# Mamba stage: GpSimd multiplies its tile of u times B by a per-partition scalar, and takes that tile in states 7, 8 and 15 too

## What is computed

```python
dt = softplus(log_dt @ W_dt.T + b_dt)                 # per position and inner channel (512)
A_bar = exp(dt[..., None] * A)                        # 16 states per inner channel
Bu = dt[..., None] * B_coef[:, :, None, :] * xc[..., None]
def step(h, inp):
    Ab, bu, c = inp
    h = Ab * h + bu
    y = einsum('bds,bs->bd', h, c)
    return (h, y)
```

## Time and profile before

| | us |
|---|---|
| median of 3 runs | 3870.74 |
| lowest and highest | 3869.91, 3874.35 |
| span of the profiled execution | 3867.2 |
| stretch of the Mamba stage in it, by first and last instructions | about 1275 to 3085 |

### The profile page before, as it was taken

One profiled execution on the slowest core, in us unless ns is written; L12 is line 12 of the kernel. 1 busy time (PEld: TensorE's weight loads), 2 busy tenths in 40 slices (PEclk: granted clock), 3 DMA queues, 4 the chain that ended last, 5 costly groups with the idle time before them and its releaser, 6 DMA issues. The chain is left out here.

```text
span 3867.2 us, 75281 instructions
## 1 busy us (share of the span) xinstructions
PE 3312.9 (86%) x23360; PEld 2499.0 (65%) x23360; DVE 3139.9 (81%) x5227; ACT 2800.4 (72%) x5125; POOL 2652.0 (69%) x2858
## 2 busy tenths in 40 slices
PE   8996989889954789898898889888888879997887
PEld 5664666667532567776776767676766757775554
DVE  5665899945395899899899989989999859998886
ACT  2223787844475888888888888888888647776997
POOL 1222677720094799999898999989999836664666
PEclk9998999979976899999999999999999989998999
DMA  2111122251113111111111111111111112221111
GB/s 65 54 55 52 45 52 50 50 116 38 41 44 84 34 51 53 57 50 52 49 56 51 56 54 48 54 51 51 56 51 48 44 48 74 73 53 56 59 56 39
DMA packets 285550, 209.64 MB, mean 54 GB/s; under 512 B 131416, under 2 KB 249752, under 8 KB 285224
## 3 DMA queue, kind: packets, MB, share of 16 engines
q1 hardware_dynamic: 285224, 205.72, 19.0%
HBM read 149.18 MB, written 51.41 MB: 52 GB/s over the span
## 5 line engine op out<-in xcount | busy, mean ns | idle before, releaser
L2896 POOL TENSOR_TENSOR ma_ch<-ma_h,ma_crep 128x512 f32<-128x512 f32 x1024 | 1368.8, 1358 | 160.0 <-DVE ma_h L2998 147.5
L2998 DVE TENSOR_TENSOR_SCAN ma_h<-ma_a,ma_pbu 128x512 f32<-128x512 f32 x1024 | 1212.7, 1206 | 172.6 <-PE ma_pbu L2576 113.0
L2576 PE MATMUL ma_pbu<-ma_ident,ma_bu 128*128 128x128 f32 x4096 | 657.7, 285 | 203.1 <-DVE ma_h L2998 161.7
L2576 PEld LDWEIGHTS ma_pbu<-ma_ident,ma_bu 128*128 128x128 f32 x4096 | 478.9, 144 | 446.1 <-DVE ma_h L2998 317.5
L2783 ACT ACTIVATE ma_a<-ma_dt,ma_A 128x510 f32<-128x510 f32 x1024 | 653.5, 718 | 1.4 <-issue 1.4
L2585 PE MATMUL ma_py<-ma_ident,ma_ch 128*128 128x128 f32 x4096 | 625.0, 279 | 0.6 <-POOL ma_ch L2896 0.6
L2774 ACT ACTIVATE ma_bu<-ma_uT,ma_b_t 128x512 f32<-128x512 f32 x784 | 508.2, 719 | 14.4 <-PE ma_pbu L2576 12.2
L2585 PEld LDWEIGHTS ma_py<-ma_ident,ma_ch 128*128 128x128 f32 x4096 | 495.8, 145 | 0.9 <-POOL ma_ch L2896 0.8
L1576 POOL TENSOR_TENSOR xa_prob<-xa_e,xa_rec_head 128x616 f32<-128x616 f32 x128 | 155.5, 1216 | 126.7 <-DVE xa_rec_head L1668 114.7
L924 POOL TENSOR_TENSOR xa_prob<-xa_e,xa_rec_head 128x616 f32<-128x616 f32 x128 | 155.5, 1216 | 108.2 <-DVE xa_rec_head L1016 90.6
L362 POOL TENSOR_TENSOR la_veps<-la_mv,la_eps 128x2 f32<-128x2 f32 x32 | 6.2, 195 | 248.2 <-DVE la_mv L395 248.2
(11 more groups left out here) (373 smaller groups left out, 8041.2 us busy)
## 6 DMA issues: line engine op xcount, KB each, us to landing
ma_crep<-ma_ct_dram SPq DMA_DIRECT2D x256, 256.0 KB
xa_x<-act SPq DMA_DIRECT2D x64, 256.0 KB, 2.6
act<-xa_y SPq DMA_DIRECT2D x64, 256.0 KB, 2.2
la_x<-in_x SPq DMA_DIRECT2D x32, 256.0 KB, 2.7
act<-la_y SPq DMA_DIRECT2D x32, 256.0 KB
act<-ea_x SPq DMA_DIRECT2D x32, 256.0 KB, 4.0
ma_x<-act SPq DMA_DIRECT2D x16, 512.0 KB, 4.5
ma_xr<-act SPq DMA_DIRECT2D x16, 512.0 KB
```

The source lines that it names most:

```text
L2576: last = pe.transpose(pbu[c % 2][:, t * P:(t + 1) * P], bu[:, s % 2, t, c * P:(c + 1) * P], ident[:, :])
L2896: pool.tensor_tensor(ch[:, s % 2, c], h[:, s % 2, c], crep[:, s % 4, :], ALU.mult).then_inc(multiplied, 1)
L2998: dve.tensor_tensor_scan(out=h[:, s % 2, c, :], data0=a[:, s % 2, c, :], data1=pbu[c % 2][:, :], initial=0.0, op0=ALU.mult, op1=ALU.add).t ...
```

## The change

Three things are changed. GpSimd's tile is made by `tensor_scalar` with a scalar from memory (times a constant 1.0) and no longer by `tensor_tensor` with a broadcast operand. The three waits ahead of the tile now stand ahead of `times_c` (s, 0) and not between it and the tile. And the tables give tile work of states 7, 8 and 15 from DVE to GpSimd: DVE has four tiles a group where it had seven, GpSimd eleven where it had eight. ACT's tiles stay as they were, two or three or four a state.

```diff
-        DVE_TILES = {1: 1, 7: 2, 8: 1, 9: 1, 10: 1, 15: 1}
-        POOL_TILES = {2: 1, 3: 1, 4: 1, 5: 1, 6: 1, 9: 1, 10: 1, 11: 1}
+        DVE_TILES = {1: 1, 7: 1, 9: 1, 10: 1}
+        POOL_TILES = {2: 1, 3: 1, 4: 1, 5: 1, 6: 1, 7: 1, 8: 1, 9: 1, 10: 1, 11: 1, 15: 1}
...
-            def scale_tile(g, par, s):
+            def tile_may_be_scaled(g, s):
                 pool.wait_ge(uT_copied, IC * g + IC)
                 pool.wait_ge(b_copied, g + 1)
                 pool.wait_ge(bu_turned, K * g + (IC * s + 4))
+
+            def scale_tile(g, par, s):
                 t = TT - 1 - DVE_TILES.get(s, 0)
-                pool.tensor_tensor(bu[:, s % 2, t, :], uT[:, par, t, :],
-                                   b_t[:, par, t, s:s + 1].broadcast_to([P, DI]), ALU.mult).then_inc(pool_tile_ready, 1)
+                pool.tensor_scalar(bu[:, s % 2, t, :], uT[:, par, t, :], b_t[:, par, t, s:s + 1], 1.0,
+                                   ALU.mult, ALU.mult).then_inc(pool_tile_ready, 1)
...
                     for c in range(IC):
+                        if c == 0 and s + 1 in POOL_TILES:
+                            tile_may_be_scaled(g, s + 1)
                         times_c(g, s, c)
                         if c == 0 and s + 1 in POOL_TILES:
                             scale_tile(g, par, s + 1)
```

## The result

The changed kernel takes 3901.1 us (median of 6 runs, 3889.9 to 3908.8) against 3870.3 us for the kernel before in the same sessions (3865.7 to 3874.4). The ratio is 1.0078, 95% interval 1.0066 to 1.0090, so it is slower by 31 us. The profiled execution took 3900.3 us with a span of 3897.3.

A forecast was written before the change was run, and what follows sets the result against it. PE was busiest over the span (86%), GpSimd in the changed stage (1649.6 of 1810 us). Terms 26.7 - 0.7 + 2 = +28 us on the 3867.2 span, plus 3.5 to the median, gave 3899 us; range 3862 to 3975.

The forecast's parts named there:

- The late tile of state 15: Behind GpSimd's step (14, 0): PE's transpose (15, 0) waits 1.78 us in 15 groups, 26.7 us; chance 0.54.
- 0.58 + X: Delay per group of PE's transpose (15, 0), waiting for GpSimd's tile; 1.78 us at the forecast's X.
- X: Duration of GpSimd's new one-input tile of 128x512: taken as 1.2 us, between 0.73 and 2.26.
- Nothing absorbs the delay afterwards: Behind transpose (15, 0): PE's `turn_u`, ACT's copy and next tiles all hang on it, so the 26.7 us stay.
- The upper row, `ff_y`: GpSimd's only earlier `tensor_scalar`, 1224 ns on 128x256 with two memory scalars; scaled up it gave X at most 2.26 us.
- The lower bound: For X: 0.73 us, from a `tensor_tensor` of 128x256 that reads the same 512 elements per partition.
- The tile of state 1: DVE's tile at a group's start, stretched beside GpSimd's step: 0.6 us on some seven groups, +2 us, ends 0 and 13.
- States 7 and 8: Tiles moved to GpSimd: DVE's later wait for rstd is hidden, since scan (8, 0) waits 2.09 us for ACT; no cost.
- The last group: DVE's 2.63 us tile goes, so GpSimd's waits of 1.49 and 0.44 us go and X comes: -0.7 us.
- GpSimd as the bound: Rival: with X at 2.26 GpSimd needs 119.3 us of a group's 113, giving 3983 us; chance 0.20.
- GpSimd caught up by (14, 0): Rival, faster: state 15's tile is in time, giving 3864 us, or 3842 if states 7 and 8 count; chance 0.18.
- That the late transpose is absorbed: Rival, nothing: PE or ACT held at the group's border by something not hanging on (15, 0), 3871 us; chance 0.08.

The follow-up runs named there:

- The early tile: The changed kernel with state 15's tile on GpSimd written behind step (13, 2) and not behind (14, 0): 3883.9 us, ratio 1.0035.
- The kernel with a subtraction: The changed kernel with GpSimd's tile subtracting the memory scalar, then multiplying by 1.0 (other values, for duration only): 3960.5 us against 3875.9 before.

## Why the prediction was right

**The late tile of state 15**, the main term: right in mechanism, 26.7 us forecast, 19.8 measured. The working was 0.58 + X. With the measured X of 0.695 it gives 1.27 us and the trace shows 1.32 per group. It was too large only because X was taken as 1.2. The early tile, with the same work on the same engines, takes this wait away, which settles that the place counts and not the load. "Nothing absorbs the delay afterwards" was too strong, though: the late tile costs the kernel 17 us with state 1's tile on DVE and 7 with it on ACT, less than the 19.8 that state 15 grows by.

**X** was wrong, outside the bounds that I had set (0.73 to 2.26). The upper row, `ff_y`, is a subtraction and tells nothing about a product of products. The lower bound, elements read per partition, is not a bound: 512 read by the new form take less than 2 x 256 by `tensor_tensor`. The estimate by the Trainium skill's "GPSIMD Engine Reference", section "Engine selection", 0.62 us by roughly line rate for one input, came nearest. It holds for this form and not for the neighbours, which take 1.56 and 2.00 us.

**The tile of state 1**, which I put at 2 us with 13 as the upper end: the mis-sized term on the other side, 14.0 us. I had named the contention and its worst price of 2.6 us, but put it at 0.6 us in some seven groups. It was 2.8 us in five: it lasted not for the GpSimd step in progress but until GpSimd ran out of work. Taking that tile off DVE removes it. So 3899 came out 2 us from the measured 3901 because an error of +7 and one of -12 met, with 3.5 us less from the last group and small differences. The direction and the main reason were right; the closeness was luck.

**States 7 and 8**: right. DVE's `finish` in front of scan (7, 0) does wait for GpSimd's rstd, and scan (8, 0) waits for ACT as before. Group 5 of the changed kernel on DVE:

```profile
1901.95 0.54 DVE L3040 TENSOR_SCALAR ma_y<-ma_pm,ma_mv,ma_rstd 128x256 f32<-128x256 f32 x1 [0.77 <-POOL ma_rstd L2916]
...
1911.11 1.22 DVE L3002 TENSOR_TENSOR_SCAN ma_h<-ma_a,ma_pbu 128x512 f32<-128x512 f32 x1 [2.10 <-ACT ma_a L2783]
```

The wait of 0.77 us on `ma_rstd` is new, the one of 2.10 us on ACT is the 2.09 of the earlier trace rows: all that happened between is covered by it. With the tile on DVE in state 15 and these two as changed, the kernel is no slower than before.

**The last group**: -0.7 forecast, -1.9 measured. The smaller X explains 0.5 of the difference; in all, states 14 and 15 gave back 3.1 us there, and state 2 took 1.2 more.

**The rivals**: GpSimd as the bound didn't occur at 0.695 us. The kernel with a subtraction, 85 us slower at 2.0 us, shows that it was a real danger. GpSimd caught up by (14, 0) didn't occur either; in the changed kernel its step (14, 0) ends before PE is let go, but only because PE waits for the tile behind it. That the late transpose is absorbed came true in part, though not by a hold at the border: the idle time of PE there, 18.0 us over the six groups that open a turn of the loop, is 18.5 in the changed kernel. It moved along with the delay, and what came back came back in other states.

## What to carry to other kernels

An engine's lag at the place where its result is needed tells more of what a moved instruction costs than its idle time in the mean: GpSimd had 10 us of idle time per group and still made everyone wait 1.3 us, since the tile stood inside its backlog. Before work is given to an engine, read how far it is behind at exactly that step, and if it is behind, write the work earlier. Where one engine's instruction can be held by another engine's, count the other one's whole unbroken run as the possible wait, not one instruction. And don't add the prices of two places before experiments have taken away each alone and then both: here 17 and 28 us went singly and 35 together.

## What was unexpected of the hardware

DVE's `tensor_scalar` of 0.46 us can be held far longer than one GpSimd instruction. It was held for 3.25 us over three, and for 4.55 to 4.63 us in the kernel with the early tile, each time until about 0.3 us after GpSimd's unbroken run ended. In state 7 the same instruction gets in after one GpSimd instruction (about 1.5 us in 13 of 16 groups of both kernels). In state 1 of the kernel before it gets in at once when it starts 1.1 us into a step of 1.28. What decides between these was not tried. GpSimd's `tensor_scalar` on 128x512 takes 0.695 us for a product with a memory scalar and a constant, 0.772 with two memory scalars, 1.564 with a single product, and 2.001 with a subtraction and a product.
